# A two-layer post-norm block with codebook look-ups: first block of x in four transfers, last down products between the norm's blocks, a ScalarE copy moved behind the one-hots

## The reference

```python
q, k, v = proj(wq), proj(wk), proj(wv)            # 32 heads of 32
q, k = rope(q), rope(k)
attn = softmax(causal(q @ k.T / sqrt(32)))
x = layernorm(x + (attn @ v) @ wo.T)
Wg, Wu = codebook[idx_gate], codebook[idx_up]     # (2752, 1024) each; codebook (16384, 8)
Wd = codebook[idx_down]                           # (1024, 2752)
x = layernorm(x + (silu(x @ Wg.T) * (x @ Wu.T)) @ Wd.T)
```

## Time and profile before

| | us |
|---|---|
| median of 3 runs | 6752.01 (6750.79 to 6754.25) |
| profiled execution | 6752.44 |
| its span, first to last instruction | 6750.5 |
| PE busy | 6615.4 (98%) |
| POOL busy | 4927.0 (73%) |
| DVE busy | 4662.0 (69%) |
| ACT busy | 3789.6 (56%) |

### The profile page before, as it was taken

One profiled execution on the slowest core, in us unless ns is written; L12 is line 12 of the kernel. 1 busy time (PEld: TensorE's weight loads), 2 busy tenths in 40 slices (PEclk: granted clock), 3 DMA queues, 4 the chain that ended last, 5 costly groups with the idle time before them and its releaser, 6 DMA issues.

```text
span 6750.5 us, 115830 instructions
## 1 busy us (share of the span) xinstructions
PE 6615.4 (98%) x29584; PEld 4063.9 (60%) x29584; DVE 4662.0 (69%) x11407; ACT 3789.6 (56%) x6692; POOL 4927.0 (73%) x5188
## 2 busy tenths in 40 slices
PE   9999899999999999999999999999999999999998
PEld 3444566666666666666666666666666666666664
DVE  3320888886776876777667776777767777677764
ACT  0000788886666755556555555555556555555552
POOL 7777777777777777777777777777777777777772
PEclk9999999999999999999999999999999999999999
DMA  4232232233333333333333333333333333333331
GB/s 140 64 90 48 56 60 55 58 80 75 82 84 74 78 72 75 65 74 73 73 68 74 76 74 73 67 74 74 72 75 67 73 73 74 74 66 73 73 71 63
DMA packets 479940, 490.59 MB, mean 73 GB/s; under 512 B 228672, under 2 KB 349248, under 8 KB 472896
## 3 DMA queue, kind: packets, MB, share of 16 engines
q10 hardware_dynamic: 298720, 425.47, 22.5%
q0 software_dynamic: 165888, 21.57, 7.8%
q1 hardware_dynamic: 14688, 36.48, 1.4%
HBM read 426.34 MB, written 56.72 MB: 72 GB/s over the span
## 4 chain that ended last, share of the span: by engine, by line
PE 75%; ACT 1%; issue 1%; DVE 0%; DMA 0%; ACTq 0%; DVEq 0%
PE ps L427 42%; PE ps L457 18%; PE ps L476 9%; PE ps L402 3%; PE ps L438 3%; PE ps L444 1%; ACT onehot L771 0%; ACT onehot L775 0%; PE ps L413 0%; PE ps L557 0%; DVE small L1068 0%; ACT arena L866 0%; DMA out_dram<-arena 0%; DVE onehot L1018 0%; DMA arena<-code_low 0%
## 5 line engine op out<-in xcount | busy, mean ns | idle before, releaser
L216 POOL DMA_INDIRECT raw<-in_codebook_dram,idx_sb x5184 | 4926.8, 950 | 1720.6 <-DMA raw<-in_codebook_dram,idx_sb 1566.8
L1018 DVE TENSOR_SCALAR_CACHE_REDUCE onehot<-arena,small 128x512 fp32r<-128x512 f32 x3845 | 2623.4, 743 | 1049.0 <-PE ps L427 998.8
L427 PE MATMUL ps<-onehot,table 128*128 128x512 f32 x12288 | 3267.6, 417 | 23.0 <-ACT onehot L775 18.7
L427 PEld LDWEIGHTS ps<-onehot,table 128*128 128x128 f32 x12288 | 2290.7, 188 | 900.1 <-issue 353.9
L771 ACT ACTIVATE onehot<-arena,small 128x512 fp32r<-128x512 f32 x2307 | 1496.7, 713 | 1139.1 <-PE ps L427 980.1
L775 ACT ACTIVATE onehot<-onehot,small 128x512 fp32r<-128x512 f32 x2307 | 1487.4, 708 | 0.0
L457 PE MATMUL ps<-big,arena 128*128 128x512 f32 x2752 | 1267.9, 597 | 0.0
L457 PEld LDWEIGHTS ps<-big,arena 128*128 128x128 f32 x2752 | 510.2, 189 | 571.7 <-issue 543.7
L1025 DVE SCALAR_TENSOR_TENSOR picked<-arena,small,ps 128x512 f32<-128x512 f16 x768 | 572.3, 745 | 158.3 <-PE ps L438 142.2
L476 PE MATMUL ps<-arena 128*128 128x512 f32 (+1 forms) x1408 | 640.4, 600 | 1.8 <-ACT arena L744 1.2
L922 DVE TENSOR_REDUCE small<-ps 128x1 f32<-128x384 f32 (+7 forms) x512 | 374.2, 752 | 270.1 <-PE ps L321 267.5
(11 more groups left out here) (74 smaller groups left out, 2726.1 us busy)
## 6 DMA issues: line engine op xcount, KB each, us to landing
arena<-code_low ACTq DMA_DIRECT2D x770, 256.0 KB
arena<-code_high ACTq DMA_DIRECT2D x770, 128.0 KB
raw<-in_codebook_dram,idx_sb POOLq DMA_INDIRECT x5184
gathered_units<-raw SPq DMA_DIRECT2D x39, 512.0 KB
arena<-gathered_units ACTq DMA_DIRECT2D x19, 1024.0 KB
queries_keys<-arena ACTq DMA_DIRECT2D x16, 1024.0 KB, 4.0
arena<-queries_keys ACTq DMA_DIRECT2D x32, 512.0 KB
big<-queries_keys ACTq DMA_DIRECT2D x32, 512.0 KB
```

The source lines that it names most:

```text
L216: pool.indirect_dma_start(raw[:, s, n, :], None, codebook, bass.IndirectOffsetOnAxis(ap=idx_sb[:, s, n:n + 1], axis=0), engine_sem=describ ...
L427: last = mm(ps[:, 4 + s % 2, :], table[:, k, c, :], onehot[:, k, :], start=(k == 0 and c == 0), stop=(k == KLO - 1 and c == PIECES - 1))
L1018: dve.tensor_scalar(onehot[:, k, :], lo_sb[:, s % 2, :], kp_sb[:, k:k + 1], None, ALU.is_equal, ALU.add, accum_out=hits[:, k:k + 1]).then_ ...
```

## The change

Three edits. The first block of x is loaded in four transfers of two k-tiles (0.5 MB) each instead of one; the matmuls wait for the quarter that they read. In steps 0 to 20 ScalarE's `take` comes behind `near` in slot 0 instead of ahead of it. In the stages of the end, the 8 down products and the 4 turns of a stage are interleaved (two downs, one turn) where before the 8 downs came first and then the 4 turns; VectorE's adds and measurings are interleaved in the same way.

```diff
@@ project_qk
                         for h in range(2):
-                            pe.wait_ge(xT_in[2 * b + h], 16)
+                            if b or h:
+                                pe.wait_ge(xT_in[2 * b + h], 16)
                             for k in range(KT):
+                                if not b and not h and k % 2 == 0:
+                                    pe.wait_ge((early_in + [xT_in[0]])[k // 2], 16)
@@ tensor, the end
             for t in range(NT + 1):
-                if t < NT:
-                    for h in range(CS):
-                        down(NTILE, t * CS + h, 2)
-                if t:
-                    for k in range(4 * t - 4, 4 * t):
-                        turn_y(k)
+                for q in range(4):
+                    if t < NT:
+                        for h in range(2 * q, 2 * q + 2):
+                            down(NTILE, t * CS + h, 2)
+                    if t:
+                        turn_y(4 * t - 4 + q)
@@ scalar, the start
-            def load_x(c):
-                act.dma_start(big1[:, :, c * N:(c + 1) * N], xT_v[:, :, c * N:(c + 1) * N]).then_inc(xT_in[c], 16)
+            def load_x(c, k0=0):
+                act.dma_start(big1[:, k0:KT, c * N:(c + 1) * N], xT_v[:, k0:KT, c * N:(c + 1) * N]).then_inc(xT_in[c], 16)
+            def load_early(q):
+                act.dma_start(big1[:, 2 * q:2 * q + 2, 0:N], xT_v[:, 2 * q:2 * q + 2, 0:N]).then_inc(early_in[q], 16)
             load_weights(0, 0)
-            load_x(0)
+            for q in range(3):
+                load_early(q)
+            load_x(0, KT - 2)
             load_weights(0, 1)
@@ scalar, lookup_step
                     next_codes(unit, unit * SLOTS, s)
-                    if s == 0:
-                        if isinstance(step, int) and step == 0:
-                            take(2, w_raw[:, 1, :])
-                        else:
-                            act.wait_ge(down_done, step * 32)
-                            take(unit - 1, d_rep)
...
                     near(unit * SLOTS, s + 1)
+                    if s == 0:
+                        if isinstance(step, int) and step == 0:
+                            take(2, w_raw[:, 1, :])
+                        else:
+                            act.wait_ge(down_done, step * 32)
+                            take(unit - 1, d_rep)
@@ vector, the end
             for t in range(NT + 1):
-                if t < NT:
-                    for h in range(CS):
-                        add(NTILE, t * CS + h, 2)
-                if t:
-                    for k in range(4 * t - 4, 4 * t):
+                for q in range(4):
+                    if t < NT:
+                        for h in range(2 * q, 2 * q + 2):
+                            add(NTILE, t * CS + h, 2)
+                    if t:
+                        k = 4 * t - 4 + q
                         measure(k)
                         if k:
                             shift(k - 1)
```

More of the change, by code:

```diff
@@ L166, in seq_post_ln_layer @@
         prep_in = sem("prep_in"); prep_step = sem("prep_step"); lo_ready = sem("lo_ready"); lo_out = sem("lo_out")
-        const_in = sem("const_in"); mask_ready = sem("mask_ready"); xT_in = [sem(f"xT_in{h}") for h in range(NT)]
+        const_in = sem("const_in"); mask_ready = sem("mask_ready"); xT_in = [sem(f"xT_in{h}") for h in range(NT)]; early_in = [sem(f"early_in{q}") for q in range(3)]
         w_in = [sem(f"w_in{m}") for m in range(2)]; wv_in = sem("wv_in")
```

## The result

| | before | changed |
|---|---|---|
| median, 11 runs of each on the same chip | 6753.58 (6750.79 to 6757.21) | 6738.34 (6734.53 to 6742.94) |
| profiled execution | 6752.44 | 6742.68 |
| its span | 6750.5 | 6740.8 |
| first down product of the last step to the end of the span | 76.3 | 61.1 |

The ratio is 0.9978, 95% interval 0.9969 to 0.9987: 15.2 us less by the medians, where 15.4 was forecast; the interval holds gains of 9 to 21 us. The profiled execution of the changed kernel is one of its slowest two, 4.3 us over the median. Its span is 9.7 us shorter than the one before: 15.2 less in the last stage, 4.0 more in the look-ups, and the look-ups start 1.4 later.

A forecast was written before the change was run, and what follows sets the result against it. TensorE, busy 98% of the span, was taken as the bound. The end's 15.2, the start's 0.2 and the steps' 0 sum to 15.4 us less: 6736.6 from 6752.01, own range 6734 to 6738.5.

The forecast's parts named there:

- The end: Last down products interleaved with the final norm's blocks: 15.2 us less, bounds 11.5 to 16.8, with VectorE the bound.
- The period: In the end, VectorE's time for one block's statistics and two adds: 3.03 us, bounds 3.0 to 3.25.
- Half clock: In the end, the last two turns were assumed at half clock, 1.94 us each.
- Rival (b): The end runs at half clock throughout: 28 us more, 6765, slower than before; chance 0.04.
- The start: First block of x in four transfers: block 1 limits the gain to 1.9 us; 0.2 taken after clock loss.
- a small term: The start's net effect, taken as a gain of 0.2 us, between 1.9 gained and 0.7 lost.
- The landing of the quarters: At the start, block 0's four transfers land at some 6.5, 12.6, 14.4 and 16.5 us.
- The 48 added waits: Three more waits within a block, again in each of 8 groups: taken as nothing, at most 2.4 us in all.
- The steps: Look-up steps, down weight's copy moved behind the one-hots: 0 in 21 steps, since nothing waits at the copy.
- Rival (c): In the look-ups, the 22 waits are the copy's and go: 18 us more gain, time 6719; chance 0.03.
- the 22 waits: TensorE's look-up waits for ScalarE's one-hots: 18.7 us in all, about 0.85 each, forecast to still stand.
- the base: Time of the kernel before from which the gain was subtracted: 6752.01 us, median of three.

The follow-up runs named there:

- the end alone: Kernel before with only the end interleaved (two downs, one turn): 6739.46 us, ratio 0.9981, 11.9 us less by the medians.
- the eight kernels at 13,200 us: Eight later kernels on two other chips, the kernel before included, with projections and attention slowed; the kernel before took 13211.09 and 13217.75 us.
- the kernel with the fourth pair of banks: Changed kernel with banks 0 and 1 as fourth pair for the last three blocks' turns: 13196.92 us, ratio 0.9990; second run 13202.88, 0.9989.

## Why the prediction was right, and where it wasn't

**The end** carries the gain, by the schedule that was written down: forecast 15.2 us less, 15.2 in the profile of the changed kernel. That close an agreement is partly luck: the same order took 60.3 to 61.5 us in other profiles, and the old order 73.5 to 76.3. Kernels in the old order have 76.3, 76.1, 75.6 and 73.5 us from the first down product, those in the new one 61.1, 61.3, 60.4, 60.4, 61.5, 60.3 and 60.4. The period was forecast at 3.03 and is 2.98; block 11's measuring begins 43.21 to 43.23 us after the first down product in all ten profiles in the new order. Half clock was put on the last two turns, and it came for part of block 14's and for all of block 15's. Part of the gain is the clock, which stays up in the new order. In the old order the four profiles have 12.5, 12.4, 10.2 and 4.4 us at half clock ahead of block 11's measuring, in the order of their times above; in the new order there is none. How the 15.2 us divide between overlap and clock no run separates.

**Rival (b)**, half clock throughout, is refuted: 1.00 for 41.5 us with a turn in each period. The Trainium skill, page "TensorE: Matmul & The Clock Gate", section "Part 4: PE-mode transpose", says that transposes don't count as busy in the same way. The eight transposes of a turn take 1.06 us at a granted 1.00 and 1.94 at 0.50, and the clock rose behind 3.75 us of nothing but turns, which speaks against it. The clock did fall each time in or behind turns, but these stand with gaps between them, and the rows don't tell the two causes apart.

**The start**: the mechanism was right, one size in it was off, and with it the sign of a small term. Block 1 ended the early start, as forecast: its first record stands at 24.6 (forecast 24.2), 1.5 us earlier than before. Behind the gap of 3.15 us the clock was at half for 3.4 us, and the 16 records of block 1 took 8.62 us instead of 6.87: 1.75 lost. In the mean of all profiles it is 1.0 gained and 2.0 lost, where 1.9 and 1.7 were put down. By the Trainium skill's rule on bursts between waits for DMA (same page, section "HAM oscillation — how this bites in real kernels") the part was worth 0 or slightly less than nothing; the trace agrees, and the rule was the better guide to the sign.

The landing of the quarters was wrong too, without effect on the time, since block 0 was through well ahead of block 1 either way. The step "So the quarters land at some 6.5, 12.6, 14.4 and 16.5 us: same bytes, same order" failed twice. The first quarter's bytes had moved at 7.3 us, not at 6.0, and the landings at 8.2, 14.4, 15.4 and 16.9 came 0.9 to 1.6 us behind the bytes (7.3, 12.8, 14.3 and 15.7), where I allowed 0.5. In the kernel before it was 1.1 (16.5 behind 15.4). Why it is that long the trace doesn't show. The 48 added waits cost nothing, as assumed: from the 33rd record to the last of queries and keys it is 425.3 us before and after.

**The steps**: nothing forecast, nothing measured, and the reason is shown from both sides: 2 us more ahead of the one-hots cost 20.1 us, behind them nothing. **Rival (c)** falls with it. What the prediction left out is GpSimd: I read its 73% and not the one load that waits for it in the second last step, which was already one of the 22 waits.

**The median**: forecast 6736.6, measured 6738.34; the gain is off by 0.2 us, the rest is the base, whose three runs had a median 1.6 us below that of eleven. The 0.2 is luck as well, since the interval is 12 us wide and the end alone measured 11.9.

## To carry to other kernels

When an engine waits for data, find the next wait behind it before counting the gain: here 8 us of earlier start ended at the same block 1, and the gap it opened cost clock. Equal counts in two lines of a profile (22 copies, 22 waits) prove nothing; look at each instance of the wait. An engine that isn't the bottleneck on average can still be late at one place, where its lead has shrunk to nothing. A stage that alternates bursts of two kinds of work gives time back when the two are interleaved and one engine is then busy throughout; its time can be worked out as that engine's period times the count.

## What the hardware did that was not expected

In the eight kernels at 13,200 us the engines ran as always at first, and were slowed until GpSimd had issued its last gather. In the second run of the kernel with the fourth pair of banks the slowing begins at 69 us, and the last gather ends at 7265. By windows, in the same run (PE, PEld, DVE, ACT, POOL busy, PEclk):

```profile
100.00:400.00 300.00, 108.17 (x108) 30.65 (x107) 19.54 (x20) 0.00 (x0) 213.06 (x223) 0.50 0.10 16
...
7300.00:8000.00 700.00, 656.60 (x7471) 435.28 (x7472) 609.48 (x1492) 585.79 (x1490) 0.00 (x0) 1.00 0.22 55
```

and its timeline:

```profile
300.85 1.01 PE L292 MATMUL ps<-big,arena 128*128 128x512 f32 x1 [1.79 <-issue]
...
303.65 1.01 PE L292 MATMUL ps<-big,arena 128*128 128x512 f32 x1 [1.79 <-issue]
303.66 0.95 POOL L221 DMA_INDIRECT raw<-in_codebook_dram,idx_sb  x1 [0.37 <-issue]
305.05 0.29 PEld L292 LDWEIGHTS ps<-big,arena 128*128 128x128 f32 x1 [2.51 <-issue]
305.07 0.94 POOL L221 DMA_INDIRECT raw<-in_codebook_dram,idx_sb  x1 [0.46 <-issue]
```

TensorE gets one matmul record every 2.80 us and GpSimd one gather every 1.40, in step, with no semaphore or transfer that the trace names as what they wait for; near 80 us TensorE had the same 2.80 while the gathers still stood 1.25 apart. 108 matmul records stand in 300 us where the profile of the kernel before has 701. Some 17 us behind the last gather the clock is at 1.00 again and all runs as always. What it is, the runs don't show. It hits every kernel alike and ends before the look-ups, so the look-ups and the end could still be read from such runs, stage by stage; what the first 60 us gain or lose can be read in the trace but not in the total.
